# Odd-tile weight products of a chunked attention moved from VectorE to GpSimd

## The reference

```python
kc = k.reshape(B, NH, C, SPLIT, HD)          # SPLIT = 64 keys per chunk, C = 16 chunks
vc = v.reshape(B, NH, C, SPLIT, HD)
scores = jnp.einsum('bhqd,bhckd->bhcqk', q, kc) * scale
w = jax.nn.softmax(scores, axis=-1)          # a softmax inside each chunk
chunk_out = jnp.einsum('bhcqk,bhckd->bhcqd', w, vc)
sum_w = w.sum(axis=-1, keepdims=True)
combined = (chunk_out * sum_w).sum(axis=2)
out = combined / (sum_w.sum(axis=2) + 1e-09)
```

## Time and profile before

| | |
|---|---|
| Median of 3 runs | 2272.51 us (2267.11 to 2275.48) |
| The profiled execution's own time | 2269.63 us |
| Its span | 2267.8 us |
| Mean granted TensorE clock | 0.922 of full speed |
| TensorE matmul busy | 1984.8 us (88%) |
| VectorE busy | 1444.2 us (64%) |
| ScalarE busy | 971.0 us (43%) |
| GpSimd busy | 572.7 us (25%) |

### The profile page before, as it was taken

How to read it: one execution, slowest core, us unless ns; L and a number is a source line. 1 busy time by engine, 2 the same in 40 slices (tenths; PEclk the granted TensorE clock), 3 DMA queues, 4 the chain that set the end, 5 groups by cost and what they waited for, 6 DMA issues and landing times.

```text
span 2267.8 us, 31835 instructions
## 1 busy us (share of the span) xinstructions
PE 1984.8 (88%) x10080; PEld 1175.0 (52%) x10080; DVE 1444.2 (64%) x2432; ACT 971.0 (43%) x1358; POOL 572.7 (25%) x543
## 2 busy tenths in 40 slices
PE   6899999996996999997768999999969889999975
PEld 3444444443783555556544444444448755555554
DVE  5678777866417776852366787778662377776432
ACT  2445444441224566551234444444413156656411
POOL 0000000000001687884120000000000037797931
PEclk7899999998887999997969999999979879999977
DMA  2366666678000000000514666666760000000015
GB/s 92 80 142 147 143 148 143 143 163 237 21 1 10 1 10 6 1 1 29 159 33 102 144 148 146 154 151 151 167 203 1 1 10 10 2 6 1 1 61 148
DMA packets 84846, 187.99 MB, mean 83 GB/s; under 512 B 17697, under 2 KB 46754, under 8 KB 83106
## 3 DMA queue, kind: packets, MB, share of 16 engines
q1 hardware_dynamic: 83650, 183.76, 32.3%
q0 software_dynamic: 1024, 2.10, 0.3%
HBM read 178.47 MB, written 8.91 MB: 83 GB/s over the span
## 4 chain that ended last, share of the span: by engine, by line
PE 61%; DVE 16%; issue 11%; ACT 6%; DMA 3%; SPq 1%; POOL 1%; DVEq 0%; ACTq 0%; POOLq 0%
PE PS L794 9%; PE PS L766 5%; PE PS L730 5%; PE PS L905 3%; PE PS L945 3%; PE PS L965 3%; DVE mx L1837 3%; PE PS L751 3%; PE PS L756 3%; PE PS L1136 3%; PE PS L948 2%; PE PS L860 2%; PE PS L1191 2%; DMA V<-weight_rows 2%; DVE mrow L1971 2%
## 5 line engine op out<-in xcount | busy, mean ns | idle before, releaser
L1837 DVE TENSOR_REDUCE mx<-PS 128x8 f32<-128x512 f32 x512 | 330.5, 685 | 181.8 <-PE PS L730 170.4
L2337 POOL TENSOR_TENSOR Esum<-Esum,EE 128x512 f32<-128x512 f32 (+3 forms) x320 | 337.5, 1084 | 16.5 <-POOL Esum L2337 10.1
L1866 DVE TENSOR_TENSOR EE<-EE,V 128x1024 f32<-128x1024 f32 x256 | 302.8, 1218 | 45.9 <-DMA V<-weight_rows 45.5
L1457 ACT ACTIVATE EE<-PS 128x1024 f32<-128x1024 f32 x256 | 260.3, 1025 | 143.3 <-PE PS L756 141.4
L2291 POOL TENSOR_TENSOR U<-xn,norm_aff 128x1024 f32<-128x1024 f32 x2 | 4.7, 2356 | 1084.0 <-DVE QA L2262 1084.0
L794 PE MATMUL PS<-EE,Vlater 128*64 128x512 f32 x1024 | 251.9, 611 | 9.1 <-ACT U L1423 8.3
L1971 DVE TENSOR_REDUCE mrow<-PS 128x1 f32<-128x512 f32 (+3 forms) x384 | 203.0, 551 | 86.7 <-PE PS L908 67.4
L730 PE MATMUL PS<-KA,QA 128*128 128x512 f32 x512 | 204.6, 451 | 33.9 <-DVE mx L1837 24.4
L751 PE MATMUL PS<-QA,KA 128*128 128x512 f32 x512 | 184.9, 442 | 0.0
L1541 ACT ACTIVATE EE<-PS 128x1024 f32<-128x1024 f32 (+2 forms) x192 | 137.8, 738 | 105.8 <-PE PS L948 103.8
L730 PEld LDWEIGHTS PS<-KA,QA 128*128 128x128 f32 x512 | 97.3, 195 | 132.8 <-DVE mx L1837 88.5
(11 more groups left out here) (306 smaller groups left out, 3310.3 us busy)
## 6 DMA issues: line engine op xcount, KB each, us to landing
V<-weight_rows SPq DMA_DIRECT2D x512, 256.0 KB, 5.5
EE<-in_w SPq DMA_DIRECT2D x48, 192.0 KB, 2.7
V<-in_Wg SPq DMA_DIRECT2D x4, 1024.0 KB, 6.3
EE<-in_Wu SPq DMA_DIRECT2D x4, 1024.0 KB, 11.4
EE<-in_Wd SPq DMA_DIRECT2D x4, 1024.0 KB, 13.4
sorted_out<-U SPq DMA_DIRECT2D x12, 256.0 KB, 3.1
wo<-in_wo SPq DMA_DIRECT2D x5, 512.0 KB, 3.9
wq_s<-in_wq SPq DMA_DIRECT2D x17, 128.0 KB, 2.9
```

The costliest lines, as they stand in the source:

```text
L1457: act.activation(EE[i % 2][:, t, :], banks(2 * (t % 2)), ACT.Exp, scale=QSCALE).then_inc(s["p2_exp"], 1)
L1837: dve.tensor_reduce(mx[:, t, half * 8:half * 8 + 8], banks(5 + x % 2, BANK).rearrange("p (c k) -> p c k", c=8), AX, ALU.max).then_inc(s["p ...
L1866: dve.tensor_tensor(EE[i % 2][:, t, :], EE[i % 2][:, t, :], weight_ring[a % 2][:, odd, :], ALU.mult).then_inc(p3_mul, 1)
L2337: ins = pool.tensor_tensor(Esum[:, h, lo:hi], Esum[:, h, lo:hi], e_tile(t)[:, h, lo - t * P:hi - t * P], ALU.add)
```

## The change

VectorE keeps the products of even tiles; the odd tiles' products are made by GpSimd, in a loop of their own over 16 heads and 4 odd tiles, in order, each after its weight tile has landed. The one semaphore `p3_mul` becomes `p3_even` and `p3_odd`; SyncE's loads and TensorE's values wait for that of their tile's kind. Two semaphores of the modulation at the start (`s_sig`, `s_rows`) become one, `s_mod_act`, with the counts 1 and 2. The data, the sizes and the order on TensorE and ScalarE stay as they are.

```diff
                             for odd in range(2):
                                 t = 2 * a + odd
                                 if i >= 1 or t >= 4:
-                                    sp.wait_ge(p3_mul, 1 + (b * HEADS + i) * NT + t - 3)
+                                    if odd:
+                                        sp.wait_ge(p3_odd, (b * HEADS + i) * (NT // 2) + a - 1)
+                                    else:
+                                        sp.wait_ge(p3_even, (b * HEADS + i) * (NT // 2) + a)
...
-                    pe.wait_ge(p3_mul, 1 + n * NT + t + 1)
+                    if t % 2:
+                        pe.wait_ge(p3_odd, n * (NT // 2) + t // 2 + 1)
+                    else:
+                        pe.wait_ge(p3_even, 1 + n * (NT // 2) + t // 2 + 1)
...
                     dve.tensor_tensor(EE[i % 2][:, t, :], EE[i % 2][:, t, :], weight_ring[a % 2][:, odd, :],
-                                      ALU.mult).then_inc(p3_mul, 1)
+                                      ALU.mult).then_inc(p3_even, 1)
...
-                        for k in range(2):
-                            if t % 2 and t >= 5 and i >= 1:
-                                weigh(i - 1, t - 5 + k)
-                            if t % 2 and t < 5 and i >= 2:
-                                weigh(i - 2, t + 3 + k)
+                        if t % 2 and t >= 5 and i >= 1:
+                            weigh(i - 1, t - 5)
+                        if t % 2 and t < 5 and i >= 2:
+                            weigh(i - 2, t + 3)
...
-                for t in range(4, NT):
+                for t in range(4, NT, 2):
                     weigh(i - 1, t)
-                for t in range(NT):
+                for t in range(0, NT, 2):
                     weigh(i, t)
...
                 pool.tensor_copy(x[:, :, :], x_next).then_inc(s_xc, 1)
+                for i in range(HEADS):
+                    for t in range(1, NT, 2):
+                        pool.wait_ge(wt_in[t % 4], ((b * HEADS + i) * 2 + t // 4 + 1) * 32)
+                        pool.sem_inc(s_held, 1)
+                        pool.tensor_tensor(EE[i % 2][:, t, :], EE[i % 2][:, t, :], weight_ring[t // 2 % 2][:, 1, :],
+                                           ALU.mult).then_inc(p3_odd, 1)
                 pool.wait_ge(xf_low, b + 1)
```

More of the change, by code:

```diff
@@ L297, in layer_program @@
         s_rest = sem("s_rest")
-        s_sig = sem("s_sig")
-        s_rows = sem("s_rows")
+        s_mod_act = sem("s_mod_act")
         s_wm = sem("s_wm")
@@ L359, in layer_program @@
         wt_in = [sem(f"wt_in{i}") for i in range(4)]
-        p3_mul = sem("p3_mul")
+        p3_even = sem("p3_even")
+        p3_odd = sem("p3_odd")
         res_link = sem("res_link")
@@ L401, in layer_program @@
         y_dn = sem("y_dn")
-        start_at_one = [s_out, s_full, xd_full, y_dn, p3_mul, xf_act, xd_out, y_up, y_silu, y_act]
+        start_at_one = [s_out, s_full, xd_full, y_dn, p3_even, xf_act, xd_out, y_up, y_silu, y_act]
         start_at_one += [S[L]["o_full"] for L in range(2)]
@@ L1346, in _ @@
             pe.wait_ge(md_link, 6)
-            pe.wait_ge(s_rows, 1)
+            pe.wait_ge(s_mod_act, 2)
             with pe.Fori(0, NB) as b:
@@ L1616, in _ @@
             act.preload_act_table_set("natural_log_exp_and_others")
-            act.activation(scol_e[:, :, :], ccol[:, :, :], ACT.Exp, scale=-1.0).then_inc(s_sig, 1)
+            act.activation(scol_e[:, :, :], ccol[:, :, :], ACT.Exp, scale=-1.0).then_inc(s_mod_act, 1)
             act.wait_ge(s_mod_ps, 2)
@@ L1621, in _ @@
                 ins = act.activation(mod[:, n, BANK:6 * P], banks(2 * n + 1, 2 * P), ACT.Copy)
-            ins.then_inc(s_rows, 1)
+            ins.then_inc(s_mod_act, 1)
             with act.Fori(0, NB) as b:
@@ L1744, in modulation @@
                 dve.wait_ge(s_c, 16)
-                dve.wait_ge(s_sig, 1)
+                dve.wait_ge(s_mod_act, 1)
                 step = Chain(dve, md_link, 0)
@@ L2280, in _ @@
         def _(pool):
-            pool.wait_ge(s_rows, 1)
+            pool.wait_ge(s_mod_act, 2)
             pool.tensor_scalar(mod[:, :, 2 * P:3 * P], mod[:, :, 2 * P:3 * P], 1.0, None, ALU.add).then_inc(s_mod, 1)
```

## The result

The changed kernel's median is 2308.27 us (2306.61 to 2318.91, 4 runs); the kernel before, run beside it, 2272.59 us. The ratio is 1.017, with a 95% interval of 1.0134 to 1.0206: slower by some 39 us (30 to 47); the two medians differ by 35.7 us. The forecast was 2287 us in a range of 2266 to 2316. The sign is that of the likeliest case and the time lies in the range, but the loss is more than twice the forecast 17 us, and the time is just above the forecast's own range of 2276 to 2306.

What follows compares the result with a forecast made beforehand. The prediction took TensorE to set the pace, with VectorE having time to spare. Its terms, -5.6 + 9.1 + 6.5 + 7.4 = +17.4 us on 2269.6 us, gave 2287 us, range 2266 to 2316.

Steps and rivals of the forecast that it cites:

- the likeliest case: Whole kernel: slower, a median above 2284 us; chance 0.48.
- Head 1: Head 1 of each pass: maxima start sooner with tile 1 on GpSimd, 2.8 us gained a pass, -5.6 us.
- The relief of steady heads: Steady heads: four products leave VectorE, 4.9 us a head, but TensorE's own scores hide it; costed at nothing.
- Step 5: Heads 2 to 14: GpSimd's tile 1 holds VectorE's tile 0 product, 0.7 us in half of 26 heads, +9.1 us.
- Steps 7 and 0: Heads 2 to 14: GpSimd's tile 7 holds L1849 for 2.0 us in one head in eight, +6.5 us.
- After the last head: End of each pass: head 15's L1849 held 2.0 us and a slower last product, 3.7 us a pass, +7.4 us.
- the larger of the two cases: Tile 7's last product on GpSimd: 2.3 us more, if VectorE's L1928 takes the port first.
- the weights of every head held: Rival: tile 7 holds L1849 in all 26 heads, 52 us in place of 6.5, 2333 us; chance 0.12.

Runs made afterwards that it cites:

- the two tiles alone: Changed kernel with GpSimd given only tiles 1 and 3 of head 0 in each pass, VectorE the others; 2259.28 us, ratio 0.9956; again 2261.72 us, 0.9967.
- the PSUM form without the last heads: Changed kernel with GpSimd's odd tiles limited to heads 0 to 13 and the normaliser's two products written to PSUM; 2271.4 us, ratio 1.0018.
- heads 13 to 15 alone: Changed kernel with GpSimd given the odd tiles of heads 13, 14 and 15 of each pass only; 2278.54 us, ratio 1.0049.
- the run with two tiles: Changed kernel with GpSimd given only tile 5 of head 14 and tile 7 of head 15 in each pass; 2278.63 us, ratio 1.0031.

## Why the prediction was right in sign and too small

Of its four terms (sum +17.4; profiled +36.8):

- **Head 1, -5.6.** Right in mechanism; that the size agrees is partly luck. The wait of 3.16 us became 0.76 and the clock there 1.00, as it said. Head 1 gives 8.1 us in the two passes. Head 0 of the first pass loses 2.1, before GpSimd's first product, for a reason that stays open, and so the two heads give 6.0 us together; the two tiles alone give 7 to 10. The relief of steady heads, costed at nothing, was next to nothing: under 1 us a pass with no odd products at all.
- **Step 5, +9.1.** Right in mechanism and nearly in count, too high in price. VectorE's product at step 5 took 2.4 us or more in 11 of the 26 heads, where 13 were taken. But step 7, in which L740 waits for the maxima behind it, became only 0.1 to 0.7 us longer in these heads, 2.7 us in all. In seven of them part of the delay falls where TensorE waited for ScalarE's copy before (0.55 us at L794); the prediction named this cover and did not price it. The six caught heads aside, heads 2 to 14 lose 5.7 us: 2.4 at this place, 2.0 by L1909 in head 13, 1.7 at step 3 of several heads and some small ones, less 1.1 that head 13 of the second pass gains. In the PSUM form without the last heads the remaining loss is 4.9 by head lengths and some 10 by medians.
- **Steps 7 and 0, +6.5.** This step failed, in size: 20.3 us by head lengths, some 24 by the run with the normaliser in PSUM. The count for tile 7 was right: one head in eight is 3.25 of 26, and three were caught. The price was wrong: 2.0 us each became 3.8 to 4.6, since TensorE, which stood for 2.74, 2.32 and 2.66 us in these heads, went on at a lower clock (0.73 from 413.5 to 418.5 us, 0.56 from 1487 to 1492, 0.50 from 1522 to 1527): the values that follow took 3.02, 3.68 and 3.68 us for 1.94. The prediction had that cost before it, in rows 11, used it for head 1's gain, and left it out of the loss. And tile 5 of a head, which it priced only at the end, caught L1855 in three more heads, which became 2.3 to 2.6 us longer. In the other heads tile 7 mostly landed after L1849's turn, as it said, but what it then met was L1860 (in 16 of 32), and L1864 only once.
- **After the last head, +7.4.** Too small: 17.1 us profiled, +11 (6 to 16) with heads 13 to 15 alone. The first part (L1855 held 2.0 us by tile 5) came with 1.0 us in the first pass, and in the second with L1864 (L1858 of before), which took 2.10 us for 0.29 and has no cover there. The last product took 3.00 us with L1933 ahead of it, as the larger of the two cases said: 1.8 us more than VectorE's, between its 1.1 and 2.3. Missing were the clock again (1.7 us at L866 in the first pass) and the odd products in between, which follow one by one with their loads: in both passes the last product ends 5.3 us later after the last head's first scores. By the end of the output product 12.3 of the 17.1 us are there (7.0 and 5.3). The rest lies in later work, which differs by several microseconds from run to run, and is not settled.

So the errors of the terms partly cancel: step 5 was some 6 us too high, steps 7 and 0 some 14 and the end some 10 too low. Two readings were a little off and change nothing: L1980 of rows 4 takes a maximum, not a product, and head 7 lasted 28.9 us, not the mean 29.2, so that L1849 was due at 291.4, as the load landed.

The mechanism is shown by two runs that alter only what it rests on: shorter GpSimd instructions (some 26 us back) and one input of two products moved to PSUM (some 24 us back). The Trainium skill (SBUF — State Buffer, Who interferes with whom) says this too, with an addition that the prediction had passed over: a VectorE instruction with one SBUF input contends as well if it runs in a 2-port mode, as an added scalar can. The trace agrees: L1860, 161 ns at the least, took 927 to 2016 in the 16 heads in which it began while a product of GpSimd ran, and at most 172 in the others; L1909 took up to 2425. Of the rivals, "the weights of every head held" was the right one to fear: six of 26 are held, and each cost 3.4 us on average where it had set 2.0.

## What to carry to other kernels

Before work goes from VectorE to GpSimd, look not at how busy VectorE is but at which of its small instructions stand in front of the bound engine, those with two SBUF inputs first and then the TENSOR_SCALARs, and when GpSimd's long instructions will start against them; one late by two microseconds can cost four. Where they meet, move one input to PSUM or cut GpSimd's instruction into pieces. And move only what stands in front of a wait: two of the 64 products of a pass gave 7 to 10 us, where leaving out all 64 gave 14.

## What the runs showed of the hardware

- The price of a TensorE wait can be more than its length. Behind 1.52 us of waiting at 557.77 us the output product took 3.78 us, behind 1.92 us in the run with two tiles 3.78 as well, at a granted clock of 0.50 (the row of stretches below); in the run with heads 13 to 15, first pass, it stood behind 1.00 us and took 2.05:

```profile
550.45 1.08 PE L813 MATMUL PS<-EE,Vlater 128*64 128x512 f32 x4 [1.00 <-POOL EE L2313]
552.82 2.05 PE L879 MATMUL PS<-wo,U 128*128 128x128 f32 x16 [1.29 <-ACT U L1442]
```

```profile
549.60:553.50 3.90, 3.78 (x16) 3.49 (x16) 0.00 (x0) 0.00 (x0) 0.00 (x0) 0.50 0.00 0
```

- A product of 1024 columns with both inputs in SBUF takes GpSimd 2.35 us, four of 256 take 4 x 0.73: some 0.19 us for each further instruction ((2.92 less 2.35) / 3).
- VectorE's reductions from PSUM (L1843) kept their pace beside GpSimd's products, 667 to 694 ns in all 512 as before (669 to 693), and a product with one input in PSUM took 289 to 290 ns in all 32 heads, while the same with both in SBUF took 280 to 2390.
